# Transformer block on one core, block products: order of ScalarE and VectorE at the batch boundary, buffers of the first weight parts

## What is computed

```
q = layer_norm(x) @ wq + bq;  k, v = context @ wk + bk, context @ wv + bv
x = x + (softmax(mask(q k^T / sqrt(32))) v) @ wo + bo        # 16 heads
h = layer_norm(x)
x = x + gelu(h @ w1 + b1) @ w2 + b2                          # w1: 512 x 2048, w2: 2048 x 512
```

## Time and profile before

| | |
|---|---|
| median of 3 runs | 3032.94 us (3029.63 to 3035.37) |
| profiled execution, its own time | 3029.86 us |
| its span, first to last instruction | 3028.1 us |
| TensorE, busy | 2815.2 us, 93% of the span |
| TensorE, weight loads | 2534.0 us, 84% |
| VectorE, busy | 2034.5 us, 67% |
| ScalarE, busy | 1650.7 us, 55% |
| GpSimd, busy | 356.2 us, 12% |
| TensorE's mean granted clock | 0.98 of 2.4 GHz |
| second stage, first product to end | 1583.70 to 3028.1 us |

### The profile page before, as it was taken

How to read it: one execution, slowest core, us unless ns; L and a number is a source line. 1 busy time by engine, 2 the same in 40 slices (tenths; PEclk the granted TensorE clock), 3 DMA queues, 4 the chain that set the end, 5 groups by cost and what they waited for, 6 DMA issues and landing times. The chain is left out here.

```text
span 3028.1 us, 65575 instructions
## 1 busy us (share of the span) xinstructions
PE 2815.2 (93%) x22056; PEld 2534.0 (84%) x22056; DVE 2034.5 (67%) x4884; ACT 1650.7 (55%) x4014; POOL 356.2 (12%) x364
## 2 busy tenths in 40 slices
PE   6999999999999999999946999999999899999999
PEld 5777777778777787777736999999999799999999
DVE  4776677766776666767647777676776766555666
ACT  3656666656666656665635545545455444444444
POOL 1211222211222112221110000000000000000000
PEclk9999999999999999999977999999999999999999
DMA  5766667666766666676522433434435334334342
GB/s 136 118 116 101 118 108 121 118 103 112 111 113 117 116 108 108 111 122 115 96 87 100 172 141 129 179 109 162 162 115 190 150 139 152 126 131 152 152 152 91
DMA packets 151738, 383.03 MB, mean 126 GB/s; under 512 B 12160, under 2 KB 16256, under 8 KB 143488
## 3 DMA queue, kind: packets, MB, share of 16 engines
q1 hardware_dynamic: 151680, 382.28, 51.6%
HBM read 172.51 MB, written 109.05 MB: 93 GB/s over the span
## 5 line engine op out<-in xcount | busy, mean ns | idle before, releaser
L711 ACT ACTIVATE sm<-sm,mins 128x128 f32<-128x128 f32 (+3 forms) x1024 | 571.6, 559 | 567.8 <-DVE mins L574 565.1
L574 DVE CUSTOM_DVE_ANT_0 sm<-bank_s,mask 128x128 f32<-128x128 f32 (+3 forms) x1024 | 480.1, 488 | 417.7 <-PE bank_s L425 407.3
L437 PE MATMUL bank_t<-ident,sm 128*128 128x128 f32 x2560 | 418.5, 278 | 73.8 <-DVE pT L520 37.4
L437 PEld LDWEIGHTS bank_t<-ident,sm 128*128 128x128 f32 x2560 | 299.5, 141 | 178.2 <-issue 58.3
L1087 PE MATMUL bank_x<-w_hi,a_hi 128*128 128x256 f32 x1024 | 302.1, 295 | 66.2 <-DVE xr L1320 43.0
L425 PE MATMUL bank_s<-stack 96*128 96x128 f32 (+3 forms) x1024 | 352.8, 385 | 6.2 <-DMA stack<-st_lo 5.8
L520 DVE COPY pT<-bank_t 128x384 f32<-128x384 f32 (+1 forms) x576 | 326.5, 567 | 1.3 <-PE bank_t L437 1.3
L1087 PE MATMUL bank_x<-b_hi,w_hi 128*128 128x256 f32 x1024 | 297.9, 291 | 15.0 <-ACT g L1478 11.2
L1089 PE MATMUL bank_x<-w_hi,a_lo 128*128 128x256 f32 x1024 | 298.8, 292 | 0.0
L1088 PE MATMUL bank_x<-w_lo,a_hi 128*128 128x256 f32 x1024 | 298.7, 292 | 0.0
L1088 PE MATMUL bank_x<-b_lo,w_hi 128*128 128x256 f32 x1024 | 292.5, 286 | 0.0
(11 more groups left out here) (179 smaller groups left out, 7393.4 us busy)
## 6 DMA issues: line engine op xcount, KB each, us to landing
stack<-st_hi SPq DMA_DIRECT2D x256, 256.0 KB, 6.1
xt<-in_x SPq DMA_DIRECT2D x32, 1024.0 KB, 5.3
stack<-st_lo SPq DMA_DIRECT2D x128, 256.0 KB, 7.2
xr<-x_scratch SPq DMA_DIRECT2D x32, 1024.0 KB, 5.7
b_scratch<-b_hi SPq DMA_DIRECT2D x16, 1792.0 KB, 10.0
b_scratch<-b_lo SPq DMA_DIRECT2D x16, 1792.0 KB, 13.7
b_hi<-b_scratch SPq DMA_DIRECT2D x16, 1792.0 KB, 7.5
b_lo<-b_scratch SPq DMA_DIRECT2D x16, 1792.0 KB, 11.2
```

Source lines behind the costliest of these rows:

```text
L437: mm = pe.transpose(bank_t[n % 2][:, P * c:P * c + P], sm[:, n % SLOTS_S, P * c:P * c + P], ident[:])
L574: op = V.tensor_tensor_reduce(sm[:, n % SLOTS_S, off:off + w], bank_s[n % BANKS_S][:, off:off + w], mask[:, 512 - w:512], 1.0, 0.0, ALU.ad ...
L711: op = A.activation(row, row, ACT.Exp, bias=mins[:, g % 2, c:c + 1], scale=-1.0, accum_out=sums[:, g % 2, c:c + 1])
```

## The change

Two things are changed in `stage_b`, and every engine but GpSimd and TensorE has new text. (1) At the end of a batch ScalarE makes both halves of operand 6 (and one half of operand 5) earlier relative to the next batch's T1, T3, T2, T4; VectorE does `sum_out(2)` and `sum_out(4)` ahead of the low parts of operands 4 and 6, and the next batch's B21, B22, T2 behind them. `h_parts` is split into `h_low` and `h_sum` for that. (2) The first phase's w2 parts have buffers of their own: part 2 in `s_sums` and a new tile `spare`, part 3 in `xr`, both loaded at the start; w1's second part is made before the first product, and in the last batch of phase 0 for phase 1. Its load now waits until the first part has landed.

```
-        OUTPUTS = [0, 2, 1, 3, 4, 5, 6]
+        OUTPUTS = [0, 2, 1, 4, 3, 5, 6]
-        raw = [g[:, 0:4, :], g[:, 4:8, :], xr, xr, xn, hT, xn, hT]
+        raw1 = {0: g[:, 0:4, :], 1: g[:, 4:8, :], 4: xn, 5: hT}
+        raw2 = {2: (sums_rows, spare), 3: (xr[:, 0:2, :], xr[:, 2:4, :]),
+                6: (xn[:, 0:2, :], xn[:, 2:4, :]), 7: (hT[:, 0:2, :], hT[:, 2:4, :])}
# SyncE, start
             sp.dma_start(xn[:], one(x_v, 0)).then_inc(xn_in, 16)
+            sp.wait_ge(raw_in[0], 32)
             load_w1(1, 0, 1)
             load_w2(2, 0, 0)
+            load_w2(3, 0, 1)
# SyncE, body
-                    raw_used(2)
-                    load_w2(3, 0, 1)
                     raw_used(3)
...
                 if ph == 1 and first:
-                    raw_used(4)
-                    load_w2(6, 1, 0)
                     raw_used(5)
                     load_w2(7, 1, 1)
...
+                if ph == 0 and last:
+                    raw_used(4)
+                    load_w2(6, 1, 0)
# VectorE, before the first body
-            for stage in range(4):
-                h_parts(0, stage)
+            w1_parts(1, 1, 0)
+            w1_parts(1, 1, 1)
+            h_low(0, "B11")
+            h_sum(0, "T1")
+            h_sum(0, "T3")
+            h_low(0, "T1")
+            h_low(0, "B21")
+            h_low(0, "B22")
+            h_sum(0, "T2")
+            w1_parts(1, 1, 2)
+            h_low(0, "T2")
+            h_sum(0, "T4")
+            w1_parts(1, 1, 3)
# VectorE, body, first part (w1_parts(U + 1, ...) taken out of four places)
                 add(c, 0, "C22")
                 if first:
+                    for stage in range(5):
+                        w2_parts(U + 2, 0, stage)
+                    if ph == 0:
+                        dve.wait_ge(w_lo_ok, 7 * 3)
                 a_sum(c, "S1", 0)
...
                 if first:
-                    w2_parts(U + 2, 0, 0)
+                    w2_parts(U + 3, 1, 0)
                 add(c, 1, "C11")
                 if first:
-                    w2_parts(U + 2, 0, 1)
+                    w2_parts(U + 3, 1, 1)
+                if switch:
+                    w1_parts(4, 0, 0)
                 add(c, 1, "C12")
                 a_low(c, 0, 1)
                 if first:
-                    w2_parts(U + 2, 0, 2)
+                    w2_parts(U + 3, 1, 2)
+                if switch:
+                    w1_parts(4, 0, 1)
# VectorE, body, end
                 a_low(c, 3, 1)
-                if norm:
-                    h_parts(c + 1, 0)
-                a_low(c, 4, 0)
-                sum_out(c, ph, 2)
+                sum_out(c, ph, 2)
+                a_low(c, 4, 0)
+                if norm:
+                    h_low(c + 1, "B11")
+                    h_sum(c + 1, "T1")
                 a_low(c, 4, 1)
                 if norm:
-                    h_parts(c + 1, 1)
+                    h_sum(c + 1, "T3")
                 a_low(c, 5, 0)
                 sum_out(c, ph, 1)
                 a_low(c, 5, 1)
-                sum_out(c, ph, 3)
-                if norm:
-                    h_parts(c + 1, 2)
+                if norm:
+                    h_low(c + 1, "T1")
+                sum_out(c, ph, 4)
                 a_low(c, 6, 0)
                 a_low(c, 6, 1)
-                sum_out(c, ph, 4)
-                if norm:
-                    h_parts(c + 1, 3)
+                if norm:
+                    h_low(c + 1, "B21")
+                    h_low(c + 1, "B22")
+                    h_sum(c + 1, "T2")
+                sum_out(c, ph, 3)
+                if norm:
+                    h_low(c + 1, "T2")
+                    h_sum(c + 1, "T4")
                 sum_out(c, ph, 5)
                 sum_out(c, ph, 6)
# ScalarE, before the first body
             w1_high(0, 0, S_HIGH)
+            w1_high(1, 1, ["A11", "A22", "A12"])
             for f, bank in enumerate((bank_x2, bank_y2, bank_z2, bank_t)):
                 x_high(0, f, bank)
+            w1_high(1, 1, ["S1", "S3"])
# ScalarE, body (w1_high(U + 1, ...) taken out of four places)
                 activate(c, ph, 0, "C12")
+                if first:
+                    w2_high(U + 2, 0, ["B11", "B21", "B22"])
                 activate(c, ph, 0, "C22")
+                if first:
+                    w2_high(U + 2, 0, ["T1", "T3", "T2", "T4"])
                 copy(c, 1, "P1")
                 activate(c, ph, 0, "C21")
                 a_high(c, 1, 0)
                 if first:
-                    w2_high(U + 2, 0, ["B11", "B21", "B22"])
+                    w2_high(U + 3, 1, ["B11", "B21", "B22"])
                 copy(c, 1, "P5")
...
                 a_high(c, 4, 1)
+                a_high(c, 5, 0)
                 if norm:
                     h_high(c + 1, "T1")
+                a_high(c, 5, 1)
+                if norm:
                     h_high(c + 1, "T3")
-                a_high(c, 5, 0)
-                a_high(c, 5, 1)
-                if norm:
-                    h_high(c + 1, "T2")
                 a_high(c, 6, 0)
                 a_high(c, 6, 1)
                 if norm:
+                    h_high(c + 1, "T2")
                     h_high(c + 1, "T4")
```

More of the change, by code:

```diff
@@ L1235, in w1_parts, with t_low @@
                     operand_low("S3")
[L1237 to L1251 removed]
+            def t_low(n, q, hi, lo, hi_ok, lo_ok, name):
+                dve.wait_ge(hi_ok, n * 7 + T_HIGH.index(name) + 1)
+                low(lo(name), q[T_AT[name]], hi(name), lo_ok)
@@ L1252, in t_parts, with t_sum @@
+            def t_sum(n, q, sum_ok, name):
+                if name == "T2":
                     dve.wait_ge(sum_ok, n * 4 + 1)
-                    V.tensor_tensor(q["B22"], q["B22"], q["B11"], ALU.subtract).then_inc(sum_ok, 1)
-                if stage == 3:
-                    operand_low("T2")
+                if name == "T4":
                     dve.wait_ge(sum_ok, n * 4 + 3)
-                    V.tensor_tensor(q["B21"], q["B21"], q["B22"], ALU.subtract).then_inc(sum_ok, 1)
-                if stage == 4:
-                    operand_low("T3")
-                    operand_low("T4")
+                left, right = {"T1": ("B12", "B11"), "T3": ("B22", "B12"), "T2": ("B22", "B11"), "T4": ("B21", "B22")}[name]
+                V.tensor_tensor(q[T_AT[name]], q[left], q[right], ALU.subtract).then_inc(sum_ok, 1)
@@ new lines, in w_sum @@
+                def w_sum(name):
+                    t_sum(u, quarters(*raw2[u]), w_sum_ok, name)
+                if stage == 0:
+                    w_low("B11")
+                    w_sum("T1")
+                    w_sum("T3")
+                if stage == 1:
+                    w_low("T1")
+                    w_low("B21")
+                if stage == 2:
+                    w_low("B22")
+                    w_sum("T2")
+                if stage == 3:
+                    w_low("T2")
+                    w_sum("T4")
@@ L1271, in add, with h_low, h_sum @@
+                if stage == 4:
+                    w_low("T3")
+                    w_low("T4")
+            def h_low(m, name):
+                t_low(m + 1, quarters(hT[:, 0:2, :], hT[:, 2:4, :]), lambda name: b_hi[:, PLACE1_B.index(name), :, :],
+                      lambda name: b_lo[:, PLACE1_B.index(name), :, :], b_hi_ok, b_lo_ok, name)
+            def h_sum(m, name):
+                t_sum(m + 1, quarters(hT[:, 0:2, :], hT[:, 2:4, :]), b_sum_ok, name)
             def add(c, d, name):
@@ L1384, in body @@
                 a_low(c, 1, 1)
-                if first:
-                    for stage in range(5):
-                        w2_parts(U + 3, 1, stage)
                 a_sum(c, "S2", 1)
@@ L1471, in h_high @@
                     act.wait_ge(b_stored, m * 32)
-                t_high(m + 1, quarters(hT), lambda name: b_hi[:, PLACE1_B.index(name), :, :], b_hi_ok, b_sum_ok, name)
+                t_high(m + 1, quarters(hT[:, 0:2, :], hT[:, 2:4, :]), lambda name: b_hi[:, PLACE1_B.index(name), :, :], b_hi_ok, b_sum_ok, name)
             def copy(c, d, name):
@@ L1508, in _ @@
             w1_high(0, 0, S_HIGH)
+            w1_high(1, 1, ["A11", "A22", "A12"])
             for f, bank in enumerate((bank_x2, bank_y2, bank_z2, bank_t)):
                 x_high(0, f, bank)
+            w1_high(1, 1, ["S1", "S3"])
             act.wait_ge(hT_ok, KT)
-            for name in T_HIGH:
+            for name in ("B11", "B21", "B22"):
                 h_high(0, name)
+            w1_high(1, 1, ["S2"])
+            for name in ("T1", "T3", "T2"):
+                h_high(0, name)
+            w1_high(1, 1, ["S4"])
+            h_high(0, "T4")
             def body(c, ph, first, last):
@@ L1574, in body @@
                     h_high(c + 1, "B22")
-                if switch:
-                    w1_high(4, 0, ["A12"])
                 a_high(c, 3, 0)
```

106 lines of the change are left out of this document (43 added, 63 removed).

## The result

The changed kernel takes 2955.98 us, the median of 4 runs (2954.98 to 2957.54), beside 3031.78 us for the kernel before. The ratio is 0.9749, with a 95% interval of 0.9732 to 0.9766: 2.5% faster, 75.8 us. The forecast was 2957. The profiled execution took 2956.78 us, with a span of 2955.1 (before: 3028.1).

The account below looks back on a forecast made before the run. In phase 0 of the second stage TensorE waits on a knot of queue orders, not engine time. 55 + 15 + 6.6 = 76 us off 3029.86 gives 2953.6, plus 3.1 to the median: 2957 us, range 2942 to 2982.

Parts of the forecast that it names:

- the term that I laid out: Start of batch 0: weight casts and VectorE operations added in front make the first product 1.8 us later.
- Ordinary batches: Batches 1 to 14 of phase 0: product 6 no longer waits, period 42.9 us; 55 us gained, bounds 42 and 62.
- Batch 0: First batch of phase 0: waits for a weight part and at product 2 go; 15 us gained, bounds 9 and 19.
- The switch: Batches 15 and 16: 43.79 becomes 41.9 and 56.72 becomes 52.0; together 6.6 us gained, bounds 1 and 10.
- One sign of being right: End of ordinary batches: ScalarE's 4.95 us of idle time before T2 are gone.
- "All of it stays and costs as much again": Ordinary batches: all the delay at the opening stays and costs as much again; the gain is 42 us, not 55.
- the new wait at its own length: Step (0,5) of ordinary batches: a new wait of 0.7 us, costed without any fall of the clock.
- The rule of the Trainium skill that I weighed: TensorE's clock: short idles between groups of products, frequent enough, make it swing; the sum would then be the clock rival's.
- The first (clock): The wait at (0,5) drops the clock, 1.58 us in ten of fourteen batches: 16 us, giving 2973; chance 0.12.
- The second (product 6 half freed): Ordinary batches: the wait at product 6 is halved, not gone; 34 us, giving 2991; chance 0.10.
- The third: Batches 0 and 16: the queue before P1, P5 and U2 takes back 20 of 21.6 us, giving 2977; chance 0.06.
- The fourth: Slower: ScalarE's B11 of the next batch waits for SP's operand store, room 5.1 us; about 3054; chance 0.04.

Follow-up runs that it names:

- e3: The kernel before with only ScalarE's order changed, its next-batch casts moved behind the a_hi; VectorE keeps its text: 2996.62 us.
- e7: The changed kernel with B11's cast and low part ahead of those of the second W1 part before batch 0: 2957.4 us.
- e10: The changed kernel without SyncE's wait for the first weight load before it issues the second, third and fourth: 2956.71 us.
- e4: The changed kernel with T2's sum and cast put back ahead of operand 6 on VectorE and ScalarE: 2983.05 us.
- e1: The kernel before with only the new order at the batch boundary on VectorE and ScalarE, weights loaded as before: 2972.76 us.
- e6: The changed kernel with two unused VectorE additions ahead of the statistics at the opening of batches 1 to 14: 2977.47 us.
- e11: The changed kernel with two unused additions and an unused bn_stats on VectorE at the opening of batches 1 to 14: 2992.1 us.
- e2: The changed kernel with the old order at the batch boundary on VectorE and ScalarE, so the buffers alone: 3017.2 us.
- e8: The changed kernel with ScalarE's copies P1 and P5 ahead of casts of the w2 parts in batches 0 and 16: 2957.56 us.
- e5: The changed kernel with VectorE's additions C11, C12 and C22 ahead of the normalise steps at a batch's opening: 2947.38 us.
- e9: The changed kernel with VectorE's additions ahead of the normalise steps only in batches 1 to 14, batch 0 kept: 2944.45 us.

## Why the prediction was right, step by step

**Where the stage begins.** The rows of the changed kernel's transposes and first product, beside 1583.70 for the first product before:

```profile
1580.62 1.08 PE L1084 MATMUL bank_x<-identb,xn 128*128 128x128 f32 x4 [25.16 <-DVE xn L1208]
...
1588.22 0.55 PE L1092 MATMUL bank_x<-b_hi,w_hi 128*128 128x256 f32 x1 [3.96 <-issue]
```

and of the kernel before:

```profile
1577.76 1.08 PE L1079 MATMUL bank_x<-identb,xn 128*128 128x128 f32 x4 [23.94 <-DVE xn L1203]
```

The first product starts 4.52 us later, not 1.8. Of that, 1.66 lie behind the transposes (7.60 instead of 5.94), which is the term that I laid out. The other 2.86 lie ahead of them. In the profiled executions of this study the transposes begin anywhere from 1575.70 (e3) to 1583.53 (e7), and e10 without the new wait has them at 1578.41, e4 with it at 1578.40: it is in the main a spread of the executions. The medians say the same: the profiled execution before was 1.9 us under its median, the one after 0.8 over, 2.7 together. A small cost is not ruled out, since the three executions with the old loads (before, e1, e3) begin at 1577.8 on average and the ten with the new ones at 1580.5. So I count from the transposes below.

**The terms.** Ordinary batches: forecast 55, measured 655.52 - 601.16 = 54.4, confirmed by e1. Batch 0: forecast 15; batch 1 started 85.38 us after the transposes and now does 69.40 after, 16.0. The switch: forecast 6.6, measured (43.79 + 56.72) - (42.01 + 52.88) = 5.6. Together 76.0, less the 2.86 of the late stage, is the 73.1 us between the two profiled executions. The forecast's sum was 76, and the medians differ by 75.8. Behind this sum stand small errors of both signs, in batch 0 and at the switch.

**Ordinary batches.** Every forecast place was met to 0.2 us or less: product 6 without a wait, the statistics 2.69 into the batch (forecast 2.7), add C22 10.07 into it (10.0), the period 42.94 (42.9). Step (0,5) is 0.68 later than before (0.7); 0.52 is only what its row shows as idle. One sign of being right did not come: ScalarE's idle time before T2 was to be gone, and 3.37 of its 4.95 us are still there. It now holds up nothing that TensorE waits for, so the time did not suffer. "All of it stays and costs as much again", the lower bound, did not come.

**The clock.** I priced the new wait at its own length, because a wait of 0.38 was followed by full speed and one of 2.37 was not; the runs now fill the gap between. A wait of 0.52 in each batch (the changed kernel), of 1.08 (e3): no slow stretch in fourteen. Of 1.72 (e6): two falls. Of 1.85 (e4): one. Of 2.31 (e11): nine. Of 2.37, in the kernel before: ten periods of 46.8 or more, as I had read from the mean, each fall worth 15.0 / 10 = 1.5 us (forecast 1.58). The ten are not scattered: they stand behind the waits of batches 2, 3, 5, 6, 7, 9, 10, 11, 13 and 14, and in e2 behind those of 1 to 3, 5, 6, 8 to 10, 12 and 13, so after two or three comes one without. "How long the wait is" is therefore not the whole rule, and what else decides stays open. The rule of the Trainium skill that I weighed ("TensorE: Matmul & The Clock Gate", section "A second HAM failure mode: psum-queue depth-cycling"), by which frequent short idles make the clock swing, gives no length and no rate for them. One idle of 0.5 us in 43, or of 1.1 and 0.4 us in 44.5, did not do it in these traces; one of 1.7 us or more in 44 to 47 did, in some batches or in most. e11 adds that nothing of product 6 is needed: at (0,5), in the other layer, a wait nearly as long as the old one brings the falls back in about as many batches.

**Batch 0.** The 9.09 us wait is gone and 0.64 for w_lo is left. Counted from the first product, (0,5) was laid out at 13.6 and came at 13.6, (1,3) at 24.8 and came at 24.0, (1,4) at 28.4 (27.7), (1,5) at 33.4 (32.5), product 2 at 46.9 (45.9), and batch 1 at 62.9 (61.8). Each place is right to about 1 us, which with a start 0.1 us earlier than laid out makes 16.0 of the forecast 15. The size agrees so well partly by luck, since with the same text batch 0 takes 60.9 to 62.8 us. e7 and e8 each took waits away, and the time stood still, so no single one of these places bounds the batch. That it is the work in the two queues together is what I conclude from that, and it is not measured by itself.

**The switch.** Here the size was off: forecast 1.9 + 4.7, measured 1.8 + 3.8. The shortfall is the length of batch 16, laid out as 52.0 and 52.88 in the trace. Of the waits laid out as 0.9, 3.1, 2.2, 2.6, 1.8 and 0.9 the rows show 0.88, 3.21, 1.92, 2.40 and 0.87; the 1.8 did not come. In its place the clock fell, to 0.94 on average, for which the sum had nothing. It does not set the length, though: the executions of e5, e9 and e6 have 0.97, 0.90 and 0.87 there, and the same 52.87 to 52.88. The waits shrink by what the products take longer, and product 2 starts 38.28 or 38.29 us into the batch in all of them, when VectorE's a_lo lets it.

**The rivals.** The first (clock) is answered by the clock of 1.00 and by e3. The second (product 6 half freed) did not happen, but e4 shows how close it stood: one pair of operations in the other order and 27 us are lost. The third is refuted by the windows and by e2, which keeps its 15.1 us. The fourth did not come: in the changed kernel the operands' store is issued at 1699.59, lands 13.5 us later, and B11 is cast at 1718.00, 4.9 us after (forecast 5.1 of room). The room before had been read as 5.8 with the median landing of 13.7; the store at 1668.24 itself landed 14.8 us later, so it was 4.7, and the change took none of it.

```profile
1699.59 0.34 SPq L1024 DMA_DIRECT2D b_scratch<-b_lo  x1
...
1718.00 1.14 ACT L1494 CAST b_hi<-hT 128x512 fp32r<-128x512 f32 x2
```

## What to carry to other kernels

Where an engine with slack still releases the busy one late, lay its queue out operation by operation: two queues that each hold the other's next input behind work for the next stage form a knot, and changing one queue alone gives only part (e3: 36 us of e1's 60). After the untying, look for the place that is late next, and put there first what the busy engine waits for; here that was worth another 11 us. The same reordering costs time where the balance is the other way round, as in batch 0, where e5 lost 2 to 3 us against e9, so treat the first pass by itself.
